# Moving the dt steps of batch 1, one SiLU, two norm-weight products, a load and two waits in a one-core layer kernel

## What is computed

```python
h = rmsnorm(x, ln1_w)
zxbcdt = h @ w_in.T                     # z (512), xs (128), Bs (128), Cs (512), dt (4 heads)
xBC = silu(causal_conv4(xBC) + conv_b)  # xs, Bs, Cs
dt = softplus(dt + dt_bias);  a = dt * -exp(A_log)
# per chunk of 128 tokens, 4 chunks to a batch:
cs   = cumsum(a);  Ldec = tril(exp(cs_q - cs_k))
Yd   = ((C @ B.T) * Ldec) @ (X * dt)
S    = exp(cs_end) * S + sum(exp(cs_end - cs) * dt * B X)      # carried from chunk to chunk
y    = (Yd + exp(cs) * C @ S_prev + D * X) * silu(z)
h    = x + y @ w_out.T
out1 = h + (silu(rmsnorm(h) @ gate.T) * (rmsnorm(h) @ up.T)) @ down.T
# the second block: a gated product with ternary weights, (x@qg.T)*(x@qu.T)@qd.T
```

## Time and profile before

| | us |
|---|---|
| median of 3 runs | 470.66 (469.86 to 471.52) |
| the profiled execution, its own time | 470.33 |
| its span in the profile | 468.6 |
| TensorE busy | 457.9 (98%) |
| VectorE busy | 340.9 (73%) |
| ScalarE busy | 259.9 (55%) |
| GpSimd busy | 222.0 (47%) |

### The profile page before, as it was taken

How to read it: one execution, slowest core, us unless ns; L and a number is a source line. 1 busy time by engine, 2 the same in 40 slices (tenths; PEclk the granted TensorE clock), 3 DMA queues, 4 the chain that set the end, 5 groups by cost and what they waited for, 6 DMA issues and landing times.

```text
span 468.6 us, 6392 instructions
## 1 busy us (share of the span) xinstructions
PE 457.9 (98%) x2078; PEld 368.2 (79%) x2078; DVE 340.9 (73%) x592; ACT 259.9 (55%) x509; POOL 222.0 (47%) x275
## 2 busy tenths in 40 slices
PE   7999999999999999999999999999999999999995
PEld 6877677876777878888788888888887777788885
DVE  3674787745788897686898999974867666587275
ACT  5798867878557767555442353322708666658000
POOL 5493555406641497777878200035028455742022
PEclk9999999999999999999999999999999999999998
DMA  6720222021322425443313347620200010000022
GB/s 206 290 90 0 92 90 69 8 90 38 91 90 90 136 67 192 149 156 113 135 51 130 136 136 225 193 76 1 90 1 0 0 47 23 1 1 1 0 91 90
DMA packets 14576, 40.81 MB, mean 87 GB/s; under 512 B 2384, under 2 KB 2640, under 8 KB 14544
## 3 DMA queue, kind: packets, MB, share of 16 engines
q1 hardware_dynamic: 14544, 40.41, 25.9%
HBM read 38.30 MB, written 2.10 MB: 86 GB/s over the span
## 4 chain that ended last, share of the span: by engine, by line
PE 82%; ACT 6%; DVE 5%; issue 2%; SPq 2%; DMA 2%; POOL 1%; POOLq 0%; DVEq 0%
PE psA L1771 7%; PE psA L1773 7%; PE psA L1786 6%; PE psA L1788 5%; PE psA L1777 4%; PE psA L1779 4%; PE psB L2024 3%; PE psB L2023 3%; PE psB L2020 3%; PE psB L1786 2%; PE psB L1788 2%; PE psB L2111 2%; PE psB L2112 2%; PE psA L2024 2%; PE psA L2020 2%
## 5 line engine op out<-in xcount | busy, mean ns | idle before, releaser
L821 POOL TENSOR_SCALAR var<-mv 128x1 f32<-128x1 f32 x16 | 4.2, 266 | 107.6 <-DVE mv L1326 103.8
L886 POOL TENSOR_TENSOR beta<-wsum,beta 128x512 fp32r<-128x512 f32 x28 | 36.2, 1314 | 21.3 <-ACT beta L1094 21.3
L1215 ACT ACTIVATE c<-c 128x512 f32<-128x512 f32 x14 | 8.8, 632 | 46.7 <-DVE c L1553 46.7
L1452 DVE SCALAR_TENSOR_TENSOR xbc<-psA,convw_sb,xbc 128x511 f32<-128x511 f32 (+2 forms) x36 | 26.9, 747 | 6.8 <-ACT xbc L1153 6.0
L1754 PE MATMUL psA<-xT_h,win_h 128*128 128x512 f32 x72 | 28.5, 402 | 0.0
L1225 ACT ACTIVATE act_hl<-act 128x512 fp32r<-128x512 f32 x28 | 17.0, 627 | 18.4 <-PE psB L2024 12.2
L1756 PE MATMUL psA<-xT_l,win_h 128*128 128x512 f32 x68 | 26.6, 391 | 0.0
L1012 POOL TENSOR_TENSOR int_l<-int,int_h 128x512 fp32r<-128x512 f32 x11 | 14.3, 1296 | 18.0 <-ACT int_h L1296 18.0
L1771 PE MATMUL psA<-xT_h,beta 128*128 128x512 f32 x56 | 22.0, 393 | 0.6 <-DVE act L1569 0.3
L1603 DVE TENSOR_TENSOR act_hl<-act,act_hl 128x512 fp32r<-128x512 f32 x28 | 19.0, 686 | 4.0 <-ACT act_hl L1225 4.0
L1773 PE MATMUL psA<-xT_l,beta 128*128 128x512 f32 x56 | 21.8, 389 | 0.0
(11 more groups left out here) (360 smaller groups left out, 1600.7 us busy)
## 6 DMA issues: line engine op xcount, KB each, us to landing
raw<-in_f_gu_t SPq DMA_DIRECT2D x22, 512.0 KB, 3.5
raw<-in_w_gu_t SPq DMA_DIRECT2D x14, 512.0 KB, 3.9
raw<-in_f_dn_t SPq DMA_DIRECT2D x10, 512.0 KB, 3.4
raw<-in_w_gu_t SPq DMA_DIRECT2D x14, 256.0 KB, 2.9
raw<-in_w_dn_t SPq DMA_DIRECT2D x7, 512.0 KB, 3.4
raw<-in_w_in_t SPq DMA_DIRECT2D x5, 512.0 KB, 5.5
x<-in_hidden SPq DMA_DIRECT2D x8, 256.0 KB, 5.4
out<-x SPq DMA_DIRECT2D x7, 256.0 KB, 2.0
```

Of the source, the lines that this page charges most:

```text
L886: nc.gpsimd.tensor_tensor(beta[:, f % 2, 1, cols], wsum[:, f % 2, cols], beta[:, f % 2, 0, cols].bitcast(F32), ALU.subtract).then_inc(gb_l ...
L1452: add = nc.vector.scalar_tensor_tensor(out=xbc[b][:, j, back:L], in0=bank_a(job)[:, 0:L - back], scalar=convw_sb[:, j, TAPS - 1 - back:TAP ...
```

## The change

It has five parts.
1. dt of batch 1: `dtturn 1` and `dtlog 1` leave their place at `inproj 0 9`, and `dtend 1` its place at `inproj 1 0`. All three now stand at `inproj 1 1`: `dtturn 1` right after `decay 0 1` and `until 0 2`, `dtlog 1` behind `conv 1 0`, `dtend 1` behind `conv 1 1`. In the round of banks "seg" of chunk 1 takes the bank of "st" of chunk 0 as before, but "st" now directly follows "seg" of chunk 0, and `dtturn 1` takes the bank of "xb" of chunk 1.
2. `silu 0 5` stands ahead of `inproj 0 7`, so that ScalarE does it before that gate's SiLU.
3. `scale1 4` stands ahead of `norm1 6`, and `scale1 5` ahead of the load that GpSimd splits.
4. The weights of the first norm are loaded after all four input tiles of batch 0, not after two, and `WARM_UP` goes from 24 to 20.
5. `p7` waits on a semaphore of its own that T3's low part raises (L1371); the wait for T4's low part goes to `p4`.

```diff
--- before.py
+++ after.py
@@ -85,14 +85,20 @@
     parts = scan_parts(0)
     for j in range(NX + NZ):
         before, after, last = parts.pop(0) if j >= NX + NZ - 2 else ([], [], [])
+        if j == NX + 1:
+
+            before = before + [("silu", 0, j - 2)]
         steps += before + [("inproj", 0, j)]
         if j == 1:
             steps.append(("dt", 0))
+
+        if j in (1, 2):
+            steps.append(("scale1", NC + j - 1))
         if j in (0, 1):
             steps += [("norm1", NC + 2 * j), ("norm1", NC + 2 * j + 1)]
         if j in (0, 2):
             steps.append(load("in", 3 + j // 2))
-        if 1 <= j <= NC:
+        if 2 < j <= NC:
             steps.append(("scale1", NC + j - 1))
         if NC <= j < NX + 1:
             steps.append(("turn1", j))
@@ -104,14 +110,12 @@
         if j == NX:
 
             steps += [("dtturn", 0), ("dtlog", 0), ("dtend", 0), ("until", 0, 0)]
-        if 2 <= j < NX + 2:
+        if 2 <= j < NX + 1:
             steps.append(("silu", 0, j - 2))
         if j in (NX + 1, NX + 2):
             steps.append(load("out", j - NX - 1))
         if j == NX + NZ - 2:
             steps.append(("dt", 1))
-        if j == NX + NZ - 1:
-            steps += [("dtturn", 1), ("dtlog", 1)]
         steps += after + [("conv", 0, j)] + last
 
     sums = [("sumgu", f) for f in range(FF)] + [("sumdn", p) for p in range(FF // 2 + 1)]
@@ -122,10 +126,16 @@
             early, middle, _ = later.pop(0)
             before, after = before + early, after + middle
         convolve = j < NX and j % 2 == 1
-        steps += before + ([("conv", 1, j - 1)] if convolve else []) + [("inproj", 1, j)] + after
-        if j == 0:
+        if j == 1:
+
+            before = before + [("dtturn", 1)]
+        steps += before + ([("conv", 1, j - 1)] if convolve else [])
+        if j == 1:
+            steps.append(("dtlog", 1))
+        steps += [("inproj", 1, j)] + after
+        steps += ([("conv", 1, j)] if convolve else []) + last
+        if j == 1:
             steps.append(("dtend", 1))
-        steps += ([("conv", 1, j)] if convolve else []) + last
         if j in (2, 4, 6):
             steps += [("silu", 1, j - 2), ("silu", 1, j - 1)]
         if j in (0, 1, 2, 3, 5, 7):
@@ -321,7 +331,7 @@
 A22_SLOTS = 3
 ACT_SLOTS = 4
 
-WARM_UP = 24
+WARM_UP = 20
 KEEP_WARM = {1: 4, 2: 2}
 IN_ON_DVE = 2
 INPROJ = [n for n, w in enumerate(LOADS) if w[0] == "in"]
@@ -565,6 +575,7 @@
         t3_ready = sem("t3_ready")
         t3_high = sem("t3_high")
         t3_low = sem("t3_low")
+        t3_mlp_low = sem("t3_mlp_low")
         t4_ready = sem("t4_ready")
         t4_high = sem("t4_high")
         t4_low = sem("t4_low")
@@ -774,9 +785,8 @@
             sources = {"in": w_in, "out": w_out, "ga": w_gu, "gb": w_gu, "dn": w_dn, "sumgu": f_gu, "qgu": f_gu, "sumdn": f_dn, "qdn": f_dn}
             for t in range(NC):
                 load_x(t)
-                if t == 1:
-
-                    sp.dma_start(ln1_sb[:], ln1_w).then_inc(ln1_loaded, 16)
+
+            sp.dma_start(ln1_sb[:], ln1_w).then_inc(ln1_loaded, 16)
             for n, (kind, *at) in enumerate(LOADS):
                 if n >= RAW_SLOTS:
 
@@ -1369,7 +1379,7 @@
                     c = at[0]
                     v.wait_ge(t_rest, c + 1)
                     nc.vector.tensor_tensor(xT_l[:, 0:2, chunk(NC + c)], t_f[:, 3],
-                                            xT_h[:, 0:2, chunk(NC + c)].bitcast(F32), ALU.subtract)
+                                            xT_h[:, 0:2, chunk(NC + c)].bitcast(F32), ALU.subtract).then_inc(t3_mlp_low, 1)
                     nc.vector.tensor_tensor(tT_l[:, 2, :, chunk(c)], t_f[:, 2],
                                             tT_h[:, 2, :, chunk(c)].bitcast(F32), ALU.subtract).then_inc(t_low, 1)
                 elif kind == "load" and LOADS[at[0]][0] == "ga":
@@ -1993,7 +2003,7 @@
                 elif kind == "p7":
 
                     f = at[0]
-                    pe.wait_ge(t_low, 2 * NC)
+                    pe.wait_ge(t3_mlp_low, NC)
                     pe.wait_ge(gb_low, 2 * f + 2)
                     product(open_a(("p74", f)), sum_weights(f, 0), moving_x(1, 0), True, None)
                 elif kind == "p3":
@@ -2003,6 +2013,7 @@
                 elif kind == "p4":
 
                     f = at[0]
+                    pe.wait_ge(t_low, 2 * NC)
                     pe.wait_ge(a22_low, f + 1)
                     pe.wait_ge(c22_ready, f + 1)
                     product(bank_a(("p74", f)), a22[:, f % A22_SLOTS], moving_t(2), False, None)
```

## The result

The changed kernel takes **471.87 us** (median of 10 runs, 471.37 to 472.47) against 469.87 us before (10 runs, 469.18 to 471.52): ratio **1.0043**, 95% interval 1.0033 to 1.0053, which is 2.0 us more (0.0043 x 469.87). Forecast were 472.6 us and a range of 469.6 to 474.0. The forecast counted from 470.66 us, the median of the first 3 runs of the kernel before; over 10 runs that median is 469.87. So the forecast change is +1.94 us, and 2.0 were measured; the forecast time lies 0.7 us above the measured one because its base did. The profiled execution took 472.33 us with a span of 470.6; the sum of the steps had been 472.45.

A forecast was written before the change was run, and what follows sets the result against it. The prediction took a VectorE-ScalarE loop as slow as TensorE to bound the kernel from 68.86 to 96 us. 470.33 + 2.64 - 0.10 - 0.42 = 472.45, given as 472.6 us for the median, range 469.6 to 474.0.

The forecast's parts named there:

- Step 1: Chunk 0, with dt work gone from its old place: `yt` 1.98 us earlier, TensorE 1.01 earlier at `inproj 1 1`.
- Step 2: VectorE ahead of `state 0 1`: thirteen small instructions, two held by GpSimd, put the state update at 67.54, +2.20 us.
- Step 3: TensorE ahead of "seg" of chunk 2 stands 2.1 us for the state update; `yt` comes 1.48 later.
- Step 4: ScalarE's Exp of chunk 2 needs a table load after the Ln and starts at 71.50, +2.64 us.
- Rival A: Loop late by half: no reload (+1.4) or small instructions slipping between GpSimd's (+1.1); 471.3 to 471.6 us; chance 0.17.
- The loop behind it: VectorE and ScalarE, Exp of chunk 2 to `turn2 0 2`: a chain without waits for TensorE, handing +2.64 us through.
- The sum for dt: Moving dt of batch 1 costs +2.64 us in all, handed through to `turn2 0 2`.
- Rival B: TensorE is the bound throughout, VectorE's new work covered: 468.8 us, needing `state 0 1` by 64.3; chance 0.13.
- Rival C: The parts cancel, the loop neither gains nor loses: -0.5, 470.1 us; chance 0.10.
- rival D: At the start the clock rises later: +1 to +2.2 us on top of the forecast, 473.6 to 474.8; chance 0.10.

The follow-up runs named there:

- exp_early: The kernel after with a one-column Exp, its result unused, behind the Ln of batch 1: 470.56 us, ratio 1.0014.
- log_no_exp: log_early without its one-column Exp behind the Ln: 469.63 us, ratio 0.9994 against the kernel before.
- log_early: Kernel before with part 5, `dtlog 1` ahead of `decay 0 1`, a one-column Exp behind its Ln, `dtend 1` behind `conv 1 4`: 468.56 us, ratio 0.9970.
- dt_alone: The kernel before with part 1 of the change, nothing else: 472.58 us, ratio 1.0054.
- log_two: log_early with parts 2 and 3 of the change as well: 468.20 us, ratio 0.9967 against the kernel before.
- two_small: The kernel before with parts 2 and 3 of the change alone: 469.86 us, ratio 1.0001.
- t3_alone: The kernel before with part 5 of the change alone: 469.26 us, ratio 0.9987.
- end_at_five: The kernel after with `dtend 1` moved behind the state update, behind `conv 1 4`: 471.05 us, ratio 1.0022 against the kernel before.
- start_alone: The kernel before with part 4 of the change alone: 469.98 us, ratio 1.0006.
- all_but_dt: The kernel before with parts 2 to 5 of the change, without part 1: 469.58 us, ratio 0.9994.
- end_five_free: end_at_five with `until 0 2` moved behind `outproj 0 0`: 469.91 us, ratio 1.0000 against the kernel before.
- warm_eight: The kernel before with part 4 of the change, but `WARM_UP` at 8: 470.47 us, ratio 1.0013.

## Why the prediction was right

**Step 1**, what comes earlier: shown. `yt` of chunk 0 is 1.75 earlier (1.80 behind the common Exp; forecast 1.98, as TensorE reached "y" at 51.80, not 51.65).

**Step 2**, thirteen small instructions that cost more than their 2.7 us: shown. They take 1.25 us (`dtturn`, 57.74 to 58.99), 1.56 (`dtlog`, 61.21 to 62.77) and 1.14 (`dtend`, 66.33 to 67.47); forecast were 1.29, 1.65 and 1.24. `dtend`'s six cost 1.16 of the scan, and the hold of an instruction by GpSimd is real: taking GpSimd's operation away took 0.73 us off L1436 and 0.74 off the scan.

Which instructions are held the rows show in part. L1424, with one operand in PSUM, runs in 0.17 under GpSimd's `ecs`; L1427 and L1436, with two operands in SBUF, are held. L1433, with a single tensor operand in SBUF, took 0.16, but it began at 61.21, only 0.08 before GpSimd's operation ended (60.25 + 1.04 = 61.29). The kernel before shows the same instruction (there L1423) further inside an operation of GpSimd, and there it is held, to 52.63 against 52.59. VectorE's and GpSimd's timelines before, 50 to 62 us:

```profile
51.91 0.72 DVE L1423 TENSOR_SCALAR dtw<-dtw 128x16 f32<-128x16 f32 x1 [0.28 <-ACT dtw L1142]
...
51.55 1.04 POOL L920 TENSOR_TENSOR until_h<-tri,adt_h 128x512 fp32r<-128x512 bf16 x1
```

So the forecast's wording, "with its operands in SBUF", stands. The Trainium skill, GPSIMD Engine Reference, section "1. Specifications", says that GpSimd shares its SBUF interfaces with VectorE and contends with VectorE instructions that have two SBUF inputs or run in a 2-port performance mode. For two inputs the trace agrees, and shows the price as the rest of GpSimd's current operation; in which mode L1423 ran no run shows.

**Step 3**, who waits: shown, with a size off. "seg" of chunk 2 starts at 68.65 (forecast 68.6). Undisturbed it would have stood at 66.50 + 0.45 = 66.95 (0.45 is the distance of the two products in the earlier trace rows, 67.56 - 67.11), so TensorE stood 1.7 us and not 2.1. TensorE was to be 1.0 us early and was 0.6; this had no effect on the end.

**Step 4**, the table load: shown twice, by taking it off the path (exp_early, 1.42) and by putting it back alone (log_no_exp against log_early, 1.12 of the scan). Rival A's first form, no reload, is against every trace here: each Exp behind a Ln had its load of 1.28 us, and the squares of `outproj` between them brought none. Its second form, small instructions that slip between GpSimd's, is against the rows of L1427 and L1436. So the rule of the Trainium skill that the prediction weighed (ScalarE: Activation LUTs, "Table sets: the hidden batching unit") does not hold in this kernel, and the measurement decides.

**The loop behind it**, from the Exp of chunk 2 to `turn2 0 2`, was to hand every shift through. It did, both ways: measured from the Exp of chunk 0, the two moved by +2.51 and +2.44 in dt_alone, +1.10 and +1.04 in exp_early, and -0.95 and -0.95 in log_early.

**The sum for dt** was +2.64 and measured +2.46 in the profile and +2.5 in the runs of dt_alone. Rival B, TensorE as the bound throughout, would have needed the state update by 64.3; it came at 67.47. In log_early and log_two it came at 63.60, and these are 1.4 and 1.6 us faster than before. An early state update alone isn't enough: in log_no_exp it came at 63.72, and the table load took all of the scan's gain (+0.17). Rival C, cancelling, is excluded by dt_alone.

**Parts 2 and 3**, worth 0 in the end: shown by two_small. The wait at the SiLU did not even go there, since TensorE came 0.75 us sooner (0.27 of it is the start of that execution) and stood for 0.29 again; in the kernel after and in log_two it is gone. The reason that the forecast gave, GpSimd's decay ahead of "y", took only a part of the gain: in two_small "y" is still 0.34 us earlier, counted from the Exp of chunk 0, and the rest went into the wait for VectorE ahead of "seg".

**Part 5**, -0.42: shown in the trace to the hundredth, and by t3_alone, -0.6 with 0.42 inside its interval (-1.0 to -0.2).

**Part 4** is the step where the working failed, at little cost. It said that the norms end at 10.4 in place of 10.64 and that 0.1 us of this goes through. The norms did end earlier. VectorE's timeline, 0 to 14 us:

```profile
7.74 2.74 DVE L1348 SCALAR_TENSOR_TENSOR xn<-x,rstd,ln_sb 128x512 f32<-128x512 f32 x4 [7.74 <-DMA ln_sb<-in_ln_w]
```

7.74 + 2.74 = 10.48 against 10.64. But what follows doesn't hang on the norms: it hangs on the DMA of the third tile of w_in. And rival D, to which the forecast gave a chance of 0.10, did occur in the profiled execution. TensorE's timeline, 0 to 24 us, and windows of 1 us:

```profile
2.80 4.00 PE L1836 MATMUL psA<-ident 128*128 128x128 f32 x20 [2.80 <-POOL strict L849]
8.55 1.52 PE L1821 MATMUL psB<-ident,xn 128*128 128x128 f32 x8 [1.75 <-DVE xn L1348]
9.86 1.06 PE L1836 MATMUL psA<-ident 128*128 128x128 f32 x4
...
15.76 1.09 PE L1913 MATMUL psA<-xT_h,win_l 128*128 128x512 f32 x4
```

```profile
9.00:10.00 1.00, 0.99 (x7) 0.79 (x6) 1.00 (x3) 0.60 (x1) 0.00 (x0) 0.77 0.65 157
10.00:11.00 1.00, 1.00 (x7) 1.00 (x6) 1.00 (x2) 0.90 (x2) 0.00 (x0) 0.50 0.95 360
```

TensorE is idle for 1.75 us, the granted clock goes from 1.00 to 0.50 (2.4 to 1.2 GHz) between 9 and 11 us, and the first product with the low weights stands at 15.76 in place of 14.22. Four transposes take 0.21 us each there (9.86 to 10.71), the sign of D that the forecast had named. Yet the Exp of chunk 0 is only 0.05 later than in before: 31.76 behind the third tile's split in place of 31.21, so 0.55 of the 1.54 us, and the split itself began 0.50 earlier. D had priced the delay at 1 to 2.2 us as if TensorE set the start; that the two cancelled in this execution is luck.

The 0.55 are TensorE's. ScalarE's copy of the third convolved tile, ScalarE's timeline, 14 to 50 us, waits for it, and the Exp of chunk 0 follows 24.45 behind, as it does before (24.43):

```profile
23.30 0.78 ACT L1163 ACTIVATE xbc<-psA,convb_sb,convw_sb 128x512 f32<-128x512 f32 x1 [0.24 <-PE psA L1774]
```

end_at_five, the other execution with slow transposes and a tail (31.48), has the same wait (0.16), and in both the Exp of chunk 0 stands 31.99 behind the first product with the low weights. The tail of start_alone (31.65) is another's: its transposes were fast, and there the fourth tile's DMA was late. Over the timed runs part 4 comes to about 0.0 to +0.3 us (0.0 from after, +0.15 from all_but_dt, +0.3 from start_alone with its interval of -0.1 to +0.7), where -0.1 was forecast.

## What to carry to other kernels

Find the instruction from which two engines hand work to each other without a pause, and price a moved step by what it puts ahead of that instruction: here thirteen tiny instructions and one table load, none of them visible in any busy time, cost 2.5 us, while of the waits removed elsewhere only that of `p7` was worth its length (0.42). Moving its cause did not remove a table load here: all fourteen traces have 17 of them. But a one-column activation placed where ScalarE is idle fetches the table ahead of time (1.42 us of the scan), and small VectorE instructions whose operands are in SBUF belong where GpSimd is idle. Before comparing two profiles, find out how much of their difference is the start of that execution (up to 0.9 us here with the same start), and measure from a common instruction behind it.

## What the runs showed of the hardware

- A 128x16 instruction of VectorE with two operands in SBUF takes 0.17 to 0.18 us, but ended only with GpSimd's operation where one was well under way: 0.92, 0.91 and 0.91 us (L1427 and L1436 of after, L1428 of end_five_free), ending within 0.03 us of it. With an operand in PSUM it takes 0.17 beside the same work. A single tensor operand in SBUF doesn't free it: L1423 of before took 0.72 us and ended 0.04 behind GpSimd's.
- An Exp behind a Ln has its own table load of 1.28 us in every trace; the activation follows right behind it (70.15 + 1.28 = 71.43, Exp at 71.44).
- The granted clock fell from 1.00 to 0.50 after 1.75 us without work at the start in the kernel after. The length of the idle time alone doesn't decide: the transposes behind it were slow (1.06 us for four) after 1.25 us of it in end_at_five, and fast (0.60 for four) after 1.24 in all_but_dt and 1.50 in start_alone. PEclk can't be trusted there: it says 1.00 from 9 to 11 us in warm_eight, where the transposes go at 0.21 to 0.22 us each in place of 0.114.
- The DMA of the third tile of w_in ends at different times from one execution to the next: its split starts at 15.69 to 16.58 in the seven with the same start, and at 17.14 in warm_eight. The Exp of chunk 0 moves with it, and from `turn2 0 2` to the end the time is again the same (374.3 us in before, dt_alone and warm_eight).
